# First causal attention of an eight-sequence stack: moved copies, a moved weighted sum, one maximum instruction for two blocks, and the splitting of the maxima on GpSimd

## What is computed

```python
q = jnp.einsum('bld,dhe->blhe', x, Wq)
k = jnp.einsum('bld,dhe->blhe', x, Wk)
v = jnp.einsum('bld,dhe->blhe', x, Wv)
a = jnp.einsum('bqhd,bkhd->bhqk', q, k) / Dh ** 0.5
a = jnp.where(mask, a, NEG_INF)          # lower triangle
a = jax.nn.softmax(a, axis=-1)
o = jnp.einsum('bhqk,bkhd->bqhd', a, v)
return jnp.einsum('blhe,hed->bld', o, Wout)
```

## Time and profile before

| | us |
|---|---|
| median of 3 runs | 933.88 |
| range of the 3 runs | 930.04 to 935.28 |
| the profiled execution, its own time | 932.55 |
| span of the profiled execution | 930.8 |
| granted PE clock, mean over the span | 0.98 |
| attention 1: first to last exponential | 396.8 to 655.4 |

### The profile page before, as it was taken

One profiled execution on the slowest core, in us unless ns is written; L12 is line 12 of the kernel. 1 busy time (PEld: TensorE's weight loads), 2 busy tenths in 40 slices (PEclk: granted clock), 3 DMA queues, 4 the chain that ended last, 5 costly groups with the idle time before them and its releaser, 6 DMA issues. The chain is left out here.

```text
span 930.8 us, 17280 instructions
## 1 busy us (share of the span) xinstructions
PE 842.5 (91%) x5977; PEld 556.6 (60%) x5977; DVE 728.3 (78%) x1455; ACT 528.7 (57%) x771; POOL 465.4 (50%) x620
## 2 busy tenths in 40 slices
PE   5899999999778886689999999888889999999997
PEld 4677777775566655334444444443558767776875
DVE  6888998879899995888898998987666656565542
ACT  4677788789566675367777777767423223222311
POOL 4133222224568786236666666456464365345444
PEclk9999999999999999779999999999989999999999
DMA  9300000000000006765545446200000000000000
GB/s 284 93 12 12 11 11 11 0 13 0 16 1 12 1 12 130 142 129 117 111 82 126 106 85 127 52 4 14 12 1 24 1 23 23 23 0 23 11 12 12
DMA packets 36067, 43.79 MB, mean 47 GB/s; under 512 B 4878, under 2 KB 28094, under 8 KB 36000
## 3 DMA queue, kind: packets, MB, share of 16 engines
q1 hardware_dynamic: 36000, 42.93, 19.5%
HBM read 21.81 MB, written 15.09 MB: 40 GB/s over the span
## 5 line engine op out<-in xcount | busy, mean ns | idle before, releaser
L1877 ACT ACTIVATE PT<-PS 128x1024 f32<-128x1024 f32 x160 | 161.5, 1022 | 61.6 <-PE PS L1668 61.3
L1939 POOL TENSOR_SCALAR_AFFINE_SELECT PT<-PT 128x256 f32<-128x256 f32 (+1 forms) x224 | 97.3, 451 | 101.9 <-ACT PT L1877 99.9
L2368 POOL TENSOR_TENSOR PRE_sb<-PRE_sb,VA 128x512 f32<-128x512 f32 x64 | 82.3, 1285 | 125.8 <-DVE PRE_sb L2436 125.7
L2335 ACT ACTIVATE sg_d<-PS 128x512 f32<-128x512 f32 x64 | 38.1, 597 | 154.5 <-PE PS L1397 154.5
L2436 DVE TENSOR_TENSOR PRE_sb<-sg_d,PS 128x512 f32<-128x512 f32 x64 | 44.0, 688 | 79.6 <-ACT sg_d L2335 79.1
L465 ACT ACTIVATE E<-PS,m 128x512 f32<-128x512 f32 x128 | 85.7, 688 | 34.7 <-PE PS L351 25.8
L1979 DVE TENSOR_REDUCE negm<-PS 128x2 f32<-128x1024 f32 x64 | 77.8, 1221 | 20.0 <-PE PS L1657 19.6
L1684 PE MATMUL PS<-PT,VA 128*32 128x512 f32 (+3 forms) x1024 | 89.9, 446 | 3.6 <-POOL PT L1939 3.6
L1650 PE MATMUL PS<-kS,qS 52*128 52x384 bf16 (+3 forms) x512 | 64.3, 311 | 14.7 <-ACT PT L1877 6.9
L514 POOL TENSOR_SCALAR Qs<-Qs 128x1024 f32<-128x1024 f32 x32 | 34.5, 1080 | 81.6 <-ACT Qs L446 81.0
L1668 PE MATMUL PS<-qS,kS 55*128 55x384 bf16 (+3 forms) x512 | 63.4, 307 | 7.5 <-DVE negm L1979 3.5
(11 more groups left out here) (331 smaller groups left out, 2249.5 us busy)
## 6 DMA issues: line engine op xcount, KB each, us to landing
qk_rows<-parts SPq DMA_DIRECT2D x32, 192.0 KB, 2.8
qS<-qk_rows SPq DMA_DIRECT2D x32, 192.0 KB, 4.3
kS<-qk_rows SPq DMA_DIRECT2D x32, 192.0 KB, 4.6
xs_sb<-XN_sb SPq DMA_DIRECT2D x20, 256.0 KB, 2.3
qk_rows<-parts SPq DMA_DIRECT2D x32, 128.0 KB, 2.8
X_sb<-in_x_dram SPq DMA_DIRECT2D x8, 256.0 KB, 6.6
qk_rows<-parts SPq DMA_DIRECT2D x32, 64.0 KB, 2.5
out_dram<-X_sb SPq DMA_DIRECT2D x8, 256.0 KB, 2.3
```

Of the source, the lines that this page charges most:

```text
L1877: nc.scalar.activation(PT[:, quad % 2, u, :], PS[:, b:b + 2, :].rearrange("p b n -> p (b n)"), ACT.Exp).then_inc(exp_ready, 1)
L1939: nc.gpsimd.affine_select(out=v, in_=v, pattern=[[0, 4 if u == 4 else 2], [1, P]], compare_op=ALU.is_ge, fill=0.0, base=0, channel_multipl ...
L2368: nc.gpsimd.tensor_tensor(acts[:, s, f, :], acts[:, s, f, :], W[:, slot, s, :], ALU.mult).then_inc(weighted, 1)
```

## The change

On PE, piece (0,) of the weighted sum moves from step u = 4 to u = 3, and the two others become one call (1, 3, 2) in step u = 1 of the next quad; `turn_ot` moves from (0, 3) and (2, 3) to (0, 4) and (2, 4), except in period 6. On ACT the copies move one exponential further back in the list. On DVE, units 2 and 3 are reduced by one instruction that gives the maxima of four 128-column blocks per bank; three of the four are later joined by one small minimum of the negated values (`join_maxima`), and `divide` moves with `turn_ot`. The splitting of the maxima moves to POOL, behind the select of (0, 0) and (2, 0), but stays on DVE for sequence 0; POOL's work on the parts of q and k and `factor` move a step further back.

```diff
 
+M_SLOT = (0, 2, 1, 3)
+
...
-        negm = sb("negm", [P, NT, 2, NPAIR])
+        negm = sb("negm", [P, NT + 3, 2, NPAIR])
...
+        def split_maxima(eng, engine, i, h):
+            ch = Steps(eng, max_steps, i * 2 + h, 4)
+            ch.n = 1
+            hs = slice(4 * h, 4 * h + 4)
+            nm, mr = negm[:, 3:7, :, hs], mrem[:, :, :, hs]
+            mp = lambda k: mpart[:, h, :, :, k, :]
+            ch.wait()
+            ch.link(engine.tensor_copy(mp(0), nm))
+            ch.link(engine.tensor_tensor(mr, nm, mp(0), ALU.subtract))
+            ch.link(engine.tensor_copy(mp(1), mr))
+            engine.tensor_tensor(mp(2), mr, mp(1), ALU.subtract).then_inc(m_parts, 1)
+            ch.end()
...
-                pe.wait_ge(masked, (i * 4 + quad) * 7 + {0: 2, 1: 6, 3: 7}[kts[0]])
+                pe.wait_ge(masked, (i * 4 + quad) * 7 + {0: 2, 1: 7}[kts[0]])
...
-                    ins = nc.tensor.transpose(tgt[:, t * P:(t + 1) * P], mpart[:, h, t, :, :, :].rearrange("p r k a -> p (r k a)"), identb[:, :])
+                    ins = nc.tensor.transpose(tgt[:, t * P:(t + 1) * P], mpart[:, h, M_SLOT[t], :, :, :].rearrange("p r k a -> p (r k a)"), identb[:, :])
...
-                    if u == 4:
+                    if u == 3:
                         weighted_v(i, slot, quad, (0,))
...
-                    elif (quad, u) == (0, 3) and not first:
+                    elif (quad, u) == ((0, 3) if opens(i, 1) else (0, 4)) and not first:
                         pe.wait_ge(m_row, i * 2 + 2)
                         turn_ot(i - 1, 1)
...
-                    elif (quad, u) == (2, 3):
+                    elif (quad, u) == ((2, 3) if opens(i, 1) else (2, 4)):
...
-                    if u == 0 or u == 1:
-                        kts = (1,) if u == 0 else (3, 2)
+                    if u == 1:
                         if quad > 0:
-                            weighted_v(i, slot, quad - 1, kts)
+                            weighted_v(i, slot, quad - 1, (1, 3, 2))
                         elif not first:
-                            weighted_v(i - 1, 1 - slot, 3, kts)
+                            weighted_v(i - 1, 1 - slot, 3, (1, 3, 2))
...
-            weighted_v(LAST, LAST % 2, 3, (1,))
-            weighted_v(LAST, LAST % 2, 3, (3, 2))
+            weighted_v(LAST, LAST % 2, 3, (1, 3, 2))
...
-                    if (quad, u) == (0, 1) and not first:
+                    if (quad, u) == (0, 2) and not first:
                         keep_ot(i - 1, 1)
-                    elif (quad, u) == (0, 2):
+                    if (quad, u) == ((0, 2) if opens(i, 1) else (0, 3)):
                         keep_maxima(i, 1)
-                    elif (quad, u) == ((1, 1) if opens(i, 1) else (1, 0)) and not (first or last):
+                    elif (quad, u) == (1, 1) and not (first or last):
                         keep_v(i + 1, 1 - slot)
-                    elif (quad, u) == (1, 2) and not first:
+                    elif (quad, u) == (1, 3) and not first:
...
-                    elif (quad, u) == (2, 0) and ahead(i):
+                    elif (quad, u) == (2, 1) and ahead(i):
                         pr.keep(act, i + 3, 0, q_ready, qf_ready)
-                    elif (quad, u) == (2, 2) and not last:
+                    elif (quad, u) == (3, 3) and ahead(i):
+                        pr.keep(act, i + 3, 1, k_ready, kf_ready)
+                    if (quad, u) == (2, 2):
+                        keep_ot(i, 0)
+                    if (quad, u) == ((2, 2) if opens(i, 1) else (2, 3)) and not last:
                         keep_maxima(i + 1, 0)
-                    elif (quad, u) == (3, 2) and ahead(i):
-                        pr.keep(act, i + 3, 1, k_ready, kf_ready)
-                    if (quad, u) == (2, 1):
-                        keep_ot(i, 0)
...
+                    if (quad, u) == (0, 0) and not first:
+                        split_maxima(pool, nc.gpsimd, i, 1)
+                    elif (quad, u) == (2, 0) and not last:
+                        split_maxima(pool, nc.gpsimd, i + 1, 0)
                     if ahead(i):
-                        if (quad, u) == (2, 0):
+                        if (quad, u) == (2, 1):
                             pr.first_part_on_pool(pool, i + 3, 0, qf_ready)
-                        elif (quad, u) == (2, 1):
+                        elif (quad, u) == (2, 2):
                             pr.first_rest(pool, i + 3, 0)
-                        elif (quad, u) == (2, 2):
+                        elif (quad, u) == (2, 3):
                             pr.second_part_on_pool(pool, i + 3, 0)
                         elif (quad, u) == (2, 4):
                             pr.third_part(pool, i + 3, 0)
-                        elif (quad, u) == (3, 2):
+                        elif (quad, u) == (3, 3):
                             pr.first_part_on_pool(pool, i + 3, 1, kf_ready)
-                        elif (quad, u) == (3, 3):
+                        elif (quad, u) == (3, 4):
                             pr.first_rest(pool, i + 3, 1)
-                        elif (quad, u) == (3, 4):
-                            pr.second_part_on_pool(pool, i + 3, 1)
                     elif (i, quad, u) in SPLIT_SLOTS:
                         n, part = divmod(SPLIT_SLOTS.index((i, quad, u)), 2)
                         (ex.low if part else ex.high)(pool, n)
-                    if (quad, u) == (1, 0) and first:
+                    if (quad, u) == (1, 1) and first:
                         factor_and_shift(nc, g, pool, 2 * LAST - 1, 2 * NB, 1, 2)
-                    elif (quad, u) == (1, 0) and i > 1:
+                    elif (quad, u) == (1, 1) and i > 1:
                         factor(i - 2)
+                    elif (quad, u) == (0, 0) and behind(i):
+                        pr.second_part_on_pool(pool, i + 2, 1)
...
-                    ins = nc.vector.tensor_reduce(negm[:, 3, :, 2 * quad + u], PS[:, b:b + 2, :], AX.X, ALU.max, negate=True)
+                    ins = nc.vector.tensor_reduce(negm[:, 3 + M_SLOT[3], :, 2 * quad + u], PS[:, b:b + 2, :], AX.X, ALU.max, negate=True)
                 elif u < 4:
                     pair = 2 * quad + u - 2
-                    nc.vector.tensor_reduce(negm[:, 2, :, pair], PS[:, b:b + 2, 0:384], AX.X, ALU.max, negate=True)
-                    ins = nc.vector.tensor_reduce(negm[:, 0, :, pair], PS[:, b:b + 2, 384:512], AX.X, ALU.max, negate=True)
+                    ins = nc.vector.tensor_reduce(negm[:, 0:4, :, pair].rearrange("p s r -> p r s"),
+                                                  PS[:, b:b + 2, :].rearrange("p b (s n) -> p b s n", n=P), AX.X, ALU.max, negate=True)
                 else:
-                    ins = nc.vector.tensor_reduce(negm[:, 1, :, 2 * quad:2 * quad + 2],
+                    ins = nc.vector.tensor_reduce(negm[:, 3 + M_SLOT[1], :, 2 * quad:2 * quad + 2],
                                                   PS[:, b:b + 2, :].rearrange("p b (r n) -> p b r n", r=2), AX.X, ALU.max, negate=True)
...
-            def split_maxima(i, h):
+            def join_maxima(i, h):
                 dve.wait_ge(max_read, i * 20 + 10 * h + 10)
-                ch = Steps(dve, max_steps, i * 2 + h, 3)
                 hs = slice(4 * h, 4 * h + 4)
-                nm, mr = negm[:, :, :, hs], mrem[:, :, :, hs]
-                mp = lambda k: mpart[:, h, :, :, k, :]
-                ch.link(nc.vector.tensor_copy(mp(0), nm))
-                ch.link(nc.vector.tensor_tensor(mr, nm, mp(0), ALU.subtract))
-                ch.link(nc.vector.tensor_copy(mp(1), mr))
-                nc.vector.tensor_tensor(mp(2), mr, mp(1), ALU.subtract).then_inc(m_parts, 1)
-                ch.end()
+                ins = nc.vector.tensor_reduce(negm[:, 3 + M_SLOT[2], :, hs], negm[:, 0:3, :, hs].rearrange("p s r a -> p r a s"), AX.X, ALU.min)
+                ins.then_inc(max_steps, 1)
...
                     if (quad, u) == (0, 0) and not first:
-                        split_maxima(i, 1)
+                        join_maxima(i, 1)
                     elif (quad, u) == (2, 0) and not last:
-                        split_maxima(i + 1, 0)
-                    if (quad, u) == (0, 3):
-                        if first:
-                            stats_of_last()
-                        else:
-                            divide(i - 1, 1)
-                    elif (quad, u) == (2, 3):
+                        join_maxima(i + 1, 0)
+                    if (quad, u) == (0, 3) and first:
+                        stats_of_last()
+                    elif (quad, u) == ((0, 3) if opens(i, 1) else (0, 4)) and not first:
+                        divide(i - 1, 1)
+                    elif (quad, u) == ((2, 3) if opens(i, 1) else (2, 4)):
                         divide(i, 0)
...
                 if u == 4 and quad % 2:
-                    split_maxima(0, quad // 2)
+                    join_maxima(0, quad // 2)
+                    split_maxima(dve, nc.vector, 0, quad // 2)
```

## The result

The changed kernel took 943.48 us in the median of 4 runs (940.34 to 945.7); the kernel before took 933.08 beside it (930.04 to 935.28). The ratio is 1.0112, with a 95% interval of 1.0072 to 1.0153: slower by 10.4 us. Predicted were 938.7, and 928 to 944 as the range. The executions of one kernel gather in groups (those of the kernel before near 929 and near 935), so a median can jump from one group to the other, and the ratio with its interval says more than a difference of medians. The profiled execution took 945.37, its span is 943.5: 12.7 more than the span before.

What follows compares the result with a forecast made beforehand. PE and DVE were both taken as nearly full, so small PE waits set the time. Terms for lead-in, periods and the very end summed to +6.2 on the profiled 932.55 us, giving 938.7, with a range of 928 to 944.

Steps and rivals of the forecast that it cites:

- rival C: At both turnings: the split on POOL is late by 0.5, 13 times; +6 us, 944; chance 0.10.
- period 7: Last period: waits before `low_rank` and `project_out`, for copies, selects and bank 7, against 1.65 gained at quad 1; +1.3 us.
- period 6: `turn_ot` stays at unit 3, both copies lie after (0,2), piece (0,) no longer covers `divide`; +0.5 us.
- the lead-in: Before attention's periods: six quicker reductions of sequence 0 by 0.17, less two joins; -0.6 us.
- Waits for DVE's product: PE before `project_v` at (1,0) and `project_out` at (3,0), one unit behind `turn_ot`: waits 0.9, twice a period.
- The short pair: Units (3,4) and (0,0), holding no other work, close the ring of bank pairs: 0.9 us lost a period.
- Nothing is saved: Weighted sum on PE: 2.57 us of matmuls a quad as before; only what covers what changes.
- POOL's four: Split of the maxima on POOL: four instructions on 32 columns, 0.22 to 0.26 each, a chain of 1.2 us.
- The copies on ACT: Copies behind the next exponential: stalls at (1,2)-(1,4) and (3,2)-(3,4) go, 1.5 us.
- Rival A: Ends of quads: old PE stalls go, new ones don't come in full; not slower, 927 us; chance 0.20.
- B: Gains and losses level out within a period, only period 7's end and the lead-in remain; 933 us, chance 0.20.
- D, the clock: Lead-in: the half-clock stretch shifts with DVE's quicker reductions, about 2 us either way; put in the range, no separate chance.

Runs made afterwards that it cites:

- experiment 2: Changed kernel with `turn_ot`, `divide` and the copy of the maxima one unit earlier (units 3; copy at 2) in every period: 940.29 us, ratio 1.007.
- experiment 11: Changed kernel with piece (0,) of quads 0 and 2 in unit 4 behind `turn_ot` in periods 1 to 5, `factor` at (1,0) in the last: 938.0 us.
- experiment 3: Changed kernel with piece (0,) of the weighted sum back in unit 4: 949.15 us, ratio 1.0186.
- experiment 6: Kernel before with only pieces (1,) and (3, 2) merged into one call at unit 1, piece (0,) staying in unit 4: 938.91 us, ratio 1.0061.
- experiment 5: Kernel before with only the merged reduction in units 2 and 3, the join, and the split of the maxima on POOL: 929.67 us, ratio 0.9987.
- experiment 7: Kernel before with only piece (0,) of the weighted sum in unit 3 for all quads: 935.41 us, ratio 1.0032.
- experiment 4: Kernel before with ACT's later copies, merged reduction, join and split on POOL; POOL's parts of q and k not moved: 937.54 us, ratio 1.0053.
- experiment 8: Kernel before with experiment 5's part, later copies for quads 1 and 3 (and v, x, `keep_on`), piece (0,) in unit 3 for those quads: 931.64 us.
- experiment 10: Experiment 9's kernel with ACT's copies of v, `keep_on`, x, q, k one exponential later; POOL's parts of q and k stay: 933.5 us, ratio 0.9999.
- experiment 1: Changed kernel with `factor` back at (1,0), ahead of POOL's select of (1,1): 941.07 us, ratio 1.0086.
- experiment 12: Kernel before with experiment 9's two edits in periods 0 to 4 alone: 930.88 us, ratio 0.9957.
- experiment 9: Kernel before with piece (0,) in unit 3 for quads 1 and 3, `factor` behind (1,1)'s select, both except in the last period: 931.35 us, ratio 0.9977.

## Why the prediction was right, and where it wasn't

- Slower was right, and the measured time lies in the range, but only by 0.5 us. It is 4.8 above the value and outside the 935 to 942 that had the chance of 0.50; the nearest number is that of rival C, whose mechanism isn't there. The forecast's sum was +6.2 in its own profile, and +12.7 came. That the total lies in the range is in part luck: periods 1 to 4 came 1.3 under their term, while period 7 came 3.8, period 6 1.5, the lead-in 1.1 and the stretch behind the last exponential 1.2 over theirs.
- Waits for DVE's product: 0.9 each forecast, 0.9 each read (the first is 0.93 at the weight load and 0.81 at the matmul). Experiments 2 and 11 put a unit or a piece between `turn_ot` and its user, and both waits go. Right.
- The short pair: 0.6 + 0.2 + 0.1 forecast; the PE rows have 0.57 at the maxima of (0,0) and 0.20 and 0.28 at the weight loads that follow. The wait is as forecast, but half of its cause isn't: experiment 3 put piece (0,) back into unit 4, and the two steps stayed at 3.3. The bare unit 0 does it, as experiment 6 shows with piece (0,) in place (3.52 instead of 2.90).
- "Nothing is saved" by one call in place of two was wrong: it gives way 0.14 sooner, 0.55 in a period. This is about what the forecast for a period was too high by (+0.65, and +0.34 came); that it is the reason wasn't isolated.
- The merged reduction (1.22 forecast, 1224 ns for it), the join (0.22, 0.17), and POOL's four (a chain of 1.2; 467.19 to 468.33) were right. For POOL the prediction set 198 ns for 4 columns against DVE's 192 for 32, which are not the same size. POOL's product of 32 columns took 0.25 where DVE's takes 0.193, 1.3 times as long; the Trainium skill (GPSIMD Engine Reference, 3.1) has the direction right, and its factor of 1.96 isn't reached at this size. That DVE's saving counts for some 0.5 in an ordinary period was wrong: experiment 5 shows 0 there, and 0.6 in period 5.
- The copies on ACT were to end 1.5 us of stalls in units 2 to 4 of quads 1 and 3. These steps did get shorter, by 0.75 and 0.60, but not through the copies: piece (0,) in unit 3 alone gives 0.66 and 0.59 (experiment 7), the later copies alone 0.16 and 0.16 (experiment 4). The prediction gave the gain to the wrong edit, and took the moved piece for a loss. The exponential that it had late at (0,3) is late there, by 0.33 (the row at 469.24); at (2,3) it isn't, because `turn_maxima` has waited 0.4 for POOL just before. What later copies cost or give by themselves no run shows, since experiments 4, 8 and 10 left POOL's list as it was. Two copies behind one exponential cost 0.49 (experiments 2 and 4).
- The largest error is period 7, +1.3 forecast, +5.1 measured. I priced `factor` behind (1,1) as a gain of 1.65 for piece (0,), and looked for what waits on POOL's selects, not for what waits on `factor`: DVE's `apply`, behind it on DVE the copy of the selection, and through it a mask on PE. Experiment 1 shows 2.8 of the 5.1, with the 1.1 that quad 1 gets from the move already set against it; the rest, 2.3, is spread over the four quads, 0.5 to 0.7 each. Of quad 2's 4.0 about half is the wait itself and half the steps at half clock behind it.
- The other terms: period 0 +0.4 (+0.3 forecast), period 5 +1.5 (+1.3), the very end +0.6 (+0.8; the merged piece waits 2.73 for the last select, where the earlier trace rows have 1.79 and 0.18). Behind the end of attention 1.3 more came in unchanged code, whose cause is open. The lead-in, -0.6 forecast, came at +0.5 with a clock of 0.96 against 0.98, and can't be judged.
- Period 6 was +0.5 forecast and +1.95 measured. 1.2 of it went together with a stretch at clock 0.5 (619.0 to 622.4): experiment 11, which has the same code in period 6, takes 35.74 without it, and the difference lies in step (2,1), 3.49 against 2.41. For the other 0.8 the merged piece is the nearest cause, since it alone costs 1.84 there (experiment 6), but the edits weren't taken apart in this period. Why the clock fell in one profile and not in the other is open.
- Rival A is excluded, and so is B; C's wait (0.5 at each turning) appears once a period, 0.4 at (2,2), where the prediction had 0.25 to spare. D, the clock, weighed more than the 2 us that I gave it, for which I had no row, and in periods 6 and 7.

## What to carry to other kernels

When an instruction moves behind another on a queue, follow its own result to the last engine that needs it, in each period that is not like the others; a few small instructions, one select later, cost one quad 4 us, half of it by the clock behind the wait. When copies move, move what reads them too, or the run tests something else. A move of matmuls between units has no price of its own: it covers a wait in one place and uncovers one in another, so try it by unit and not for all at once (33.44 for all quads, 32.33 for two). Time taken off DVE, which is 78% busy over the span and 91% in an ordinary period, bought nothing in such a period and 0.6 in period 5: a busy share doesn't tell which wait ends last.

## What the hardware showed

The same code took different times by where the clock fell. Up to the first exponential the kernel before and the one of experiment 10 have the same instructions:
```profile
0.00:396.80 396.80, 341.02 (x1895) 254.78 (x1895) 341.58 (x743) 266.93 (x423) 180.24 (x190) 0.98 0.18 45
```
```profile
0.00:392.60 392.60, 341.73 (x1895) 255.68 (x1895) 338.53 (x743) 266.39 (x423) 178.52 (x190) 0.98 0.18 45
```
4.2 us apart at the same mean clock. In experiment 10 one stretch at about half the clock (1.2 GHz, granted 0.51) lies over 384 to 401 us:
```profile
384.00:401.00 17.00, 12.18 (x112) 5.67 (x112) 16.23 (x26) 7.72 (x10) 6.96 (x11) 0.51 0.80 167
```
What a slow stretch costs shows best in period 7 of experiment 12: 3.4 us at clock 0.5 made step (1,4) 1.15 longer than in the kernel before, with the same code. Whole executions follow the mean clock: of the twelve of experiment 12 the four at 0.980 and 0.981 took 925.2 to 926.8 us, the others (0.968 to 0.976) 930.6 to 935.2.

In the changed kernel PE stood still for 2.44 us, and half the clock was granted from 653.1 to 659.9, behind that pause. Experiments 2 and 3, which leave `factor` where the change puts it, have waits of 1.5 and 2.4 for the selection and slow stretches of 3.4 us behind them; experiments 1 and 11, which put it back, have waits of 0.3 and less and no such stretch in the last period. But the pause is not the only way to a slow stretch: experiments 5, 7, 8 and 12 have one of 3.4 us in the last period with `factor` at (1,0).

DVE's small instructions are slower beside POOL's. In experiment 10, where POOL's cast of 512 columns and its product run at the same time, the last three of DVE's four instructions of a split took 0.53, 0.31 and 0.33; in experiment 9, 0.19, 0.18 and 0.19. DVE's reductions from PSUM kept their 1.22 beside POOL in both.

With 29 runs of the kernel before between 928.34 and 938.67, differences of a few us in one execution say little; the periods of the steady part (33.24 four times, 32.33 four times) are what can be compared.
